# Mask rows that seed the score banks: written two banks at a time, and shared out otherwise between ScalarE and VectorE

## The reference

```
scores  = q @ k.T + mask[b]          # 512 x 1024, the mask is float32, the same for all heads
weights = softmax(scores)
out     = weights @ v                # v is the context as well
```

## Time and profile before

| | |
|---|---|
| three runs, median | 5450.16 us |
| lowest and highest | 5443.2 and 5451.83 us |
| profiled execution, span from first to last instruction | 5453.5 us |
| mean granted clock of PE in it, share of 2.4 GHz | 0.883 |
| busy in the span: PE, DVE, ACT, POOL | 4470.3, 3008.7, 2794.5, 1691.7 us |
| masked attention: first fill to last instruction of the stage | 4817 to 5341 us |

### The profile page before, as it was taken

One profiled execution on the slowest core, in us unless ns is written; L12 is line 12 of the kernel. 1 busy time (PEld: TensorE's weight loads), 2 busy tenths in 40 slices (PEclk: granted clock), 3 DMA queues, 4 the chain that ended last, 5 costly groups with the idle time before them and its releaser, 6 DMA issues. The chain is left out here.

```text
span 5453.5 us, 72915 instructions
## 1 busy us (share of the span) xinstructions
PE 4470.3 (82%) x20471; PEld 2052.5 (38%) x20471; DVE 3008.7 (55%) x6900; ACT 2794.5 (51%) x5841; POOL 1691.7 (31%) x1362
## 2 busy tenths in 40 slices
PE   8779663847799956794898899999998869669986
PEld 5322553745322255323343233333334544312223
DVE  4567564036488522677653555555552247558875
ACT  3447221322366722472444477777774226339993
POOL 2112141121201111121442477777775111300001
PEclk9679876978799977896999899999999889769998
DMA  8544102520823254542545544444430055644421
GB/s 301 137 106 111 54 2 63 189 79 1 283 52 95 56 202 157 175 111 85 184 175 195 128 105 100 102 103 109 109 91 18 34 161 129 206 132 108 109 62 37
DMA packets 534966, 634.87 MB, mean 116 GB/s; under 512 B 84644, under 2 KB 441748, under 8 KB 522180
## 3 DMA queue, kind: packets, MB, share of 16 engines
q1 hardware_dynamic: 527168, 595.62, 38.7%
q0 software_dynamic: 6384, 32.61, 1.9%
q10 hardware_dynamic: 1068, 2.66, 0.2%
HBM read 399.52 MB, written 217.45 MB: 113 GB/s over the span
## 5 line engine op out<-in xcount | busy, mean ns | idle before, releaser
L828 POOL TENSOR_TENSOR la_core_weight_sums<-la_core_weight_sums,la_core_weights 128x1024 f32<-128x1024 f32 x320 | 752.3, 2351 | 140.2 <-ACT la_core_weights L693 132.6
L734 DVE TENSOR_REDUCE la_core_part_max<-ps 128x1 f32<-128x512 f32 x768 | 518.9, 681 | 499.6 <-PE ps L560 499.0
L630 PE MATMUL ps<-la_core_q,la_core_k 128*128 128x512 bf16 x2304 | 624.5, 382 | 13.5 <-ACT ps L676 10.3
L693 ACT ACTIVATE la_core_weights<-ps 128x512 f32<-128x512 f32 x768 | 455.5, 593 | 293.3 <-PE ps L630 293.3
L218 POOL TENSOR_TENSOR proj_parts<-proj_rest,proj_parts 128x512 bf16<-128x512 f32 x240 | 303.8, 1273 | 663.5 <-ACT proj_parts L169 663.0
L676 ACT ACTIVATE ps<-la_core_tops 128x512 f32<-128x512 f32 x768 | 460.3, 599 | 57.9 <-DMA la_core_tops<-la_core_max_rows 57.9
L593 PE MATMUL ps<-la_core_weights,la_core_v 128*64 128x512 f32 x1536 | 414.0, 617 | 0.0
L630 PEld LDWEIGHTS ps<-la_core_q,la_core_k 128*128 128x128 bf16 x2304 | 195.0, 98 | 485.1 <-ACT ps L676 302.5
L734 DVE TENSOR_REDUCE l1x_core_part_max<-ps 128x1 f32<-128x512 f32 x512 | 316.7, 681 | 83.7 <-PE ps L558 77.1
L206 DVE CAST proj_parts<-proj_full 128x512 bf16<-128x512 f32 x240 | 168.0, 700 | 313.8 <-ACT proj_full L181 158.2
L730 DVE CUSTOM_DVE_ANT_0 l3x_core_unused<-ps,l3x_core_mask_q 128x512 f32<-128x512 f32 x512 | 330.6, 686 | 7.4 <-DVE l3x_core_row_max L738 4.9
(11 more groups left out here) (460 smaller groups left out, 8487.2 us busy)
## 6 DMA issues: line engine op xcount, KB each, us to landing
la_core_k<-latent_k_parts SPq DMA_DIRECT2D x128, 384.0 KB
latent_k_parts<-proj_parts SPq DMA_DIRECT2D x96, 384.0 KB, 2.6
cf_w<-in_L1f_w SPq DMA_DIRECT2D x32, 1024.0 KB, 6.9
values<-proj_value SPq DMA_DIRECT2D x112, 256.0 KB, 3.1
latent_values<-proj_value SPq DMA_DIRECT2D x96, 256.0 KB, 3.0
la_core_q<-latent_q_parts SPq DMA_DIRECT2D x192, 128.0 KB
la_core_v<-latent_values SPq DMA_DIRECT2D x32, 768.0 KB, 5.5
k_parts<-proj_parts SPq DMA_DIRECT2D x56, 384.0 KB, 2.6
```

What stands on the lines that cost most here:

```text
L630: mm = nc.tensor.matmul(out, k_stack[r][:, kp, j, ks], q_stack[r][:, p, j, qs], start=False, stop=False, skip_group_check=True)
L693: nc.scalar.activation(weights[:, (g * NS + s) % WEIGHTS, qs], k.ps[:, B0 + (g * NS + s) % B_BANKS, qs], ACT.Exp, scale=scale).then_inc(ex ...
L734: nc.vector.reduce_max(out, scores, AX).then_inc(a_taken, 1)
L828: nc.gpsimd.tensor_tensor(total, total, own, ALU.add).then_inc(added, 1)
```

## The change

Where there is a mask, a fill now covers a pair of neighbouring banks (`per_fill` = 2): one instruction writes the mask rows of a key tile, read twice, over two banks. A group has 16 pairs (`NF`); pair u is for the steps 2u and 2u + 1, which belong to the same key tile. DVE has the pairs with u modulo 8 in 1, 4 and 6, ACT the others. `fill_after` replaces `step_after`: it gives nothing at odd s and pair s / 2 + 1 at even s, which is filled after exponential s - 1 as before. Ahead of the loops only pair 0 is filled, by ACT; DVE's fills there are gone. PE waits for a pair at its first step alone. The attentions without a mask keep one bank a fill and their lead of `LEAD`.

```diff
--- before.py
+++ after.py
@@ -304,12 +304,17 @@
         return [some[len(some) * j // heads:len(some) * (j + 1) // heads] for j in range(heads)]
 
     assert not seeded or groups * NS % B_BANKS == 0 and groups * NCH % A_BANKS == 0
-    by_vector = [s for s in range(NS) if mask is not None and s % 4 == 1]
-    by_scalar = [s for s in range(NS) if s not in by_vector]
-
-    def step_after(b, g, s):
-
-        return (b, g, s + LEAD) if s + LEAD < NS else (b + (g + 1) // groups, (g + 1) % groups, s + LEAD - NS)
+    per_fill = 2 if mask is not None else 1
+    NF = NS // per_fill
+    by_vector = [u for u in range(NF) if mask is not None and u % 8 in (1, 4, 6)]
+    by_scalar = [u for u in range(NF) if u not in by_vector]
+
+    def fill_after(b, g, s):
+
+        if s % per_fill:
+            return None
+        u = s // per_fill + (LEAD if per_fill == 1 else 1)
+        return (b, g, u) if u < NF else (b + (g + 1) // groups, (g + 1) % groups, u - NF)
 
     with ExitStack() as held:
         def sb(what, shape, dt):
@@ -615,10 +620,12 @@
                     qs, ks = queries_of(i), slice(i * P, (i + 1) * P)
                     for j in range(heads):
                         s = i * heads + j
-                        if s in by_vector:
-                            pe.wait_ge(filled_by_vector, at(b, g, len(by_vector), by_vector.index(s) + 1))
-                        elif seeded:
-                            pe.wait_ge(filled, at(b, g, len(by_scalar), by_scalar.index(s) + 1))
+                        u = s // per_fill
+                        if seeded:
+                            if s % per_fill == 0 and u in by_vector:
+                                pe.wait_ge(filled_by_vector, at(b, g, len(by_vector), by_vector.index(u) + 1))
+                            elif s % per_fill == 0:
+                                pe.wait_ge(filled, at(b, g, len(by_scalar), by_scalar.index(u) + 1))
                         else:
                             pe.wait_ge(exp_done, at(b, g, NS, 3 if g == s == 0 else s + 1))
                         out = k.ps[:, B0 + (g * NS + s) % B_BANKS, qs]
@@ -663,23 +670,25 @@
                     out = sums[:, g % SUMS, :]
                 nc.scalar.activation(out, k.ps[:, ACC, 0:nq], ACT.Copy).then_inc(acc_copied, 1)
 
-            def fill(b, g, s):
-
+            def fill(b, g, u):
+
+                bank = B0 + (g * NS + u * per_fill) % B_BANKS
                 if mask is not None:
+                    i = u * per_fill // heads
                     if g == 0:
-                        act.wait_ge(mask_k_in[s // heads // 2], 16 * (b + 1))
-                    seed = mask_k[:, s // heads, :]
+                        act.wait_ge(mask_k_in[i // 2], 16 * (b + 1))
+                    out, seed = k.ps[:, bank:bank + per_fill, 0:nq], mask_k[:, i, :].unsqueeze(1).broadcast_to((P, per_fill, nq))
                 else:
-                    if s == 0:
+                    if u == 0:
                         act.wait_ge(row_in, 16 * at(b, g, 1, 1))
-                    seed = tops[:, g % 2, s % heads, :]
-                nc.scalar.activation(k.ps[:, B0 + (g * NS + s) % B_BANKS, 0:nq], seed, ACT.Copy).then_inc(filled, 1)
+                    out, seed = k.ps[:, bank, 0:nq], tops[:, g % 2, u % heads, :]
+                nc.scalar.activation(out, seed, ACT.Copy).then_inc(filled, 1)
 
             if seeded:
                 act.wait_ge(opened, B_BANKS)
-                for s in range(LEAD):
-                    if s in by_scalar:
-                        fill(0, 0, s)
+                for u in range(LEAD if per_fill == 1 else 1):
+                    if u in by_scalar:
+                        fill(0, 0, u)
 
             def group(b, g):
                 for s in range(NS):
@@ -692,8 +701,8 @@
                     act.wait_ge(s_ready, at(b, g, NS, s + 1))
                     nc.scalar.activation(weights[:, (g * NS + s) % WEIGHTS, qs], k.ps[:, B0 + (g * NS + s) % B_BANKS, qs], ACT.Exp, scale=scale
                                          ).then_inc(exp_done, 1)
-                    after = step_after(b, g, s)
-                    if seeded and after[2] in by_scalar and exists(*after[:2]):
+                    after = fill_after(b, g, s) if seeded else None
+                    if after and after[2] in by_scalar and exists(*after[:2]):
                         act.wait_ge(exp_done, at(b, g, NS, s + 3))
                         fill(*after)
                     if s == heads - 1 and exists(*later(b, g, -1)):
@@ -750,12 +759,14 @@
                     dve.wait_ge(row_in, 16 * at(b, g, 1, 0))
                 nc.vector.tensor_scalar(negative[:, g % 2, :], k.ps[0:slots, SIDE, 0:P], -1.0, None, ALU.mult).then_inc(negated, 1)
 
-            def fill(b, g, s, exponentiated):
-
+            def fill(b, g, u, exponentiated):
+
+                bank, i = B0 + (g * NS + u * per_fill) % B_BANKS, u * per_fill // heads
                 if g == 0:
-                    dve.wait_ge(mask_k_in[s // heads // 2], 16 * (b + 1))
+                    dve.wait_ge(mask_k_in[i // 2], 16 * (b + 1))
                 dve.wait_ge(exp_done, exponentiated)
-                nc.vector.tensor_copy(k.ps[:, B0 + (g * NS + s) % B_BANKS, 0:nq], mask_k[:, s // heads, :]).then_inc(filled_by_vector, 1)
+                nc.vector.tensor_copy(k.ps[:, bank:bank + per_fill, 0:nq], mask_k[:, i, :].unsqueeze(1).broadcast_to((P, per_fill, nq))
+                                      ).then_inc(filled_by_vector, 1)
 
             def invert_dense(b):
                 dve.wait_ge(dense_in, 16 * (b + n_carried + 1))
@@ -771,9 +782,6 @@
 
             if by_vector:
                 dve.wait_ge(opened, B_BANKS)
-                for s in range(LEAD):
-                    if s in by_vector:
-                        fill(0, 0, s, 1)
             maxima(0, 0, range(NCH))
             negate(0, 0)
             maxima(0, 1, range(NCH))
@@ -783,8 +791,8 @@
                 for i in range(nkt):
                     more = chunks_of(i) if exists(*later(b, g, 2)) else [()] * heads
                     for j in range(heads):
-                        after = step_after(b, g, i * heads + j)
-                        if after[2] in by_vector and exists(*after[:2]):
+                        after = fill_after(b, g, i * heads + j) if by_vector else None
+                        if after and after[2] in by_vector and exists(*after[:2]):
                             fill(*after, at(b, g, NS, i * heads + j + 3))
                         maxima(*later(b, g, 2), more[j])
                         if (i, j) in inverse_at and not small and exists(*before):
```

## The result

| | before | after |
|---|---|---|
| median | 5449.9 us (4 runs) | 5508.7 us (4 runs) |
| lowest and highest | 5443.2, 5451.8 | 5504.5, 5516.2 |
| profiled execution, span | 5453.5 | 5503.2 |

The ratio is 1.0111, with a 95% interval from 1.0097 to 1.0125: 58.8 us slower. The two profiled executions differ by only 49.7 us. The sublayers ahead of this stage, equal in both, ended 8.6 us earlier in the one of after (the stage's first matmul started at 4793.69 for 4802.32). So what follows compares stretches of the stage itself.

The account below looks back on a forecast made before the run. ACT's pace was taken as the bound; +65 us in 14 groups, +5 in the last two and -9 at the start gave +61 on 5453.5, 5514, less 3.3 for the median: 5511 us, own range 5485 to 5540, widened to 5475 to 5548.

Parts of the forecast that it names:

- What bounds the kernel now: 14 groups with maxima: ACT's pace, 57 instructions of 0.50 us, 28.5 us a group; 13.2 us in all are stalls.
- the ring: Fill, score, exponential, next fill two steps later: 15.6 us a 16-step block without queueing, against 14.0 now.
- What the change removes: Fills: two-bank ones last 1.03 us on ACT, 1.23 on DVE; ACT's work falls to 25.8 us a group.
- What it moves: Masked attention's fills: lead falls from three steps to two, both banks of a pair waiting for the later exponential.
- the timetable: A 16-step block written out from DVE's fill at 0, with queueing behind maxima and weighing: 16.5 us.
- The signs: 14 groups: ACT near 80% busy, exponentials waiting 0.9 us behind DVE fills, DVE's fills waiting 0.3 to 0.7 us.
- The rule of the Trainium skill on rotating banks: Score banks: independent matmul groups should rotate through different banks; pairs make two units of four, so the change costs time.
- The sum: Whole stage: +65 us in 14 groups, +5 in the last two, -9 at the start, +61 us.
- The start: Stage start: DVE's first maximum no longer stands behind a fill waiting for the key mask, -9.3 us.
- Throughput: Rival for the stage: queues absorb latencies, so the slower engine sets the pace and it becomes faster; 5432 us, chance 0.08.
- Two-bank fills save nothing: Rival on fills: held 1.00 and 1.24 us, they make the ring 16.2 us a block; 5530 us, chance 0.08.
- The clock: Rival: TensorE's clock falls through PE's gaps, 4.5 us a block in a third of blocks; 5556 us, chance 0.06.

Follow-up runs that it names:

- the order turned: Changed kernel with ACT's two-bank fill placed ahead of exponential s instead of behind it, its waits kept: 5454.9 us, ratio to before 1.0011.
- the run with it alone: Kernel before with DVE's first fill moved behind the first group's maxima: 5442.1 us, ratio 0.9986.
- the fastest version: Kernel before with DVE's first fill behind the first group's maxima and three one-bank fills in four by DVE in the last two groups: 5421.3 us, ratio 0.9951.
- the share spread evenly: Kernel before, one-bank fills and three-step lead kept, DVE given 12 fills a group at steps 1, 4, 6 of 8: 5470.8 us, ratio 1.0040.

## Why the prediction was right

- **What bounds the kernel now**: right. Its quiet groups take 28.7 us, and ACT's pace is 28.5. What I missed is the next bound, close under it: the cycle over maxima, chunk matmul, weighing and score, 27.7 us a group with DVE's 8 fills and near 30 with the changed kernel's share. It didn't decide here, since the ring is longer (32.9 us a group), so the forecast stood.
- **What the change removes**: right. The two-bank fills lasted 1.02 and 1.23 us as extended from the rows by width, and against two single fills they save 19 us.
- **What it moves, and the ring**: right. The block is 16.32 us for 16.47 by the timetable, the steps before agree within 0.05 us, and with the order turned 54 of the 59 us go. The signs came too: ACT busy 379 of 469 us (81%), exponentials that wait 0.63 to 0.89 us behind a DVE fill, DVE's fills that wait 0.27 to 0.58 us for an exponential. The link over a DVE fill without a row (0.05 us from its end to the score) was 4936.34 - 4936.28 = 0.06. The rule of the Trainium skill on rotating banks ("Perfetto Trace Analysis", Optimizing Tensor Performance) agrees in its direction: with the same banks on each engine, one-bank instructions in pairs took 33.7 us a group for 31.5 singly. It isn't the whole: with pairs kept and only the order turned, a group took 30.0.
- **The sum**: its two halves were each mis-sized, and the errors cancelled, which is luck: -9 and +6.5 us. The 14 groups grew by 56 us and not 65. Of these 9 us, 4 are the block (32.9 for 33.15 a group, 14 times). The rest is the stalls at the turns of the loop, which I took to be 13.2 us and to stay: the kernel before has 412.5 - 14 x 28.7 = 11 us of them, the changed one 468.8 - 14 x 32.9 = 8. The last two groups grew by 11.5 us and not 5: I had kept the clock at 1.00 there, and it fell to 0.76, which is 5 of the 6.5 us.
- **The start**: right, -9.4 us for -9.3 in the trace, and in the run with it alone the first maximum came as early.
- **Rivals.** *Throughput* falls, and its own figure was off: even with the ring opened the kernel is at 5455 us and not 5432, for the most part because of the second cycle. The rule on the fixed cost of an instruction ("VectorE: DVE Perf Modes", The TRN2 errata, in the Trainium skill) holds for the instruction here (1.02 us on ACT for two banks, against 0.60 for one), as the 19 us show, and says nothing of the waits that come with it. *Two-bank fills save nothing* falls by their durations; the forecast for it, 5530, is near what two one-bank fills did (5528). *The clock* came in part: I had given it a third of all blocks, between the two kernels it differs in the last two groups only, for 5 us.

## What to carry to other kernels

Before widening an instruction that refills a buffer, write out who waits for whom around one buffer: a wider refill has to wait for the last reader of all its buffers, and where the next user stands only two steps on, the latencies of refill, use and handoff are exposed once a pair. Saved busy time on the bound engine is then worth only what it takes out of that ring (19 us here), while the place of the refill in its engine's order can be worth nearly all of the loss (54 of 59 us). A share moved to an engine with idle time costs its time where that engine's result gates a queue, as the maxima gate the weighing here.

## What I had not expected of the hardware

In the last two groups of the changed kernel PE was busy 48.3 of 70.2 us, and the granted clock fell to 0.50 (1.2 GHz) three times, for some 34 us in all, 0.76 in the mean. The first of these stretches and what came between it and the next:

```profile
...
5328.00:5348.30 20.30, 16.29 (x54) 1.98 (x50) 3.89 (x4) 13.42 (x22) 2.71 (x3) 0.50 0.00 1
5348.50:5358.60 10.10, 5.62 (x35) 1.05 (x34) 2.46 (x2) 8.69 (x15) 0.00 (x0) 1.00 0.00 0
...
```

With two one-bank fills for each pair these two groups took 74.1 us at a mean of 0.73, with all pairs on ACT 81.7 us at 0.56. In the kernel before the clock was 0.91 there, and in the fastest version 1.00 in the stretch shown. One matmul more a step brought it to 1.00 (2.4 GHz), and the stretch got 5 us shorter though PE had more to do. What differs is PE's activity in these groups: scores come in pairs with a gap after them. I didn't test what of it the clock goes by. A short fall in a group that is otherwise quiet costs 1.1 to 1.3 us (31.45 for 30.2 with the share spread evenly, 34.9 for 33.7 with two one-bank fills).
